# A fused decoder layer on one core: rotations by neighbour DMA and GpSimd, masks by ScalarE and GpSimd, half of the convolution's taps as matmuls

## The reference, cut to what matters

```python
# block 1 (state space), D_INNER = 256, D_STATE = 16
x_b, z = split(x @ W_in)
xc = silu(conv_b + sum_k xpad[:, k:k+T, :] * conv_w[:, k])       # four taps, causal, within a sequence
delta = softplus(proj[..., :8] @ W_dt + b_dt); B_in, C_in = proj[..., 8:24], proj[..., 24:]
h = exp(delta * A) * h + delta * B_in * xc                       # a scan over T, per channel and state
y = (sum_s h * C_in + D_param * xc) * silu(z); x1 = layernorm(x + y @ W_out)
# block 2 (retention): queries from x1, keys and values from ctx
rot(u) = stack(-u[1::2], u[0::2]); q = (x1 @ Wq) * cos + rot(x1 @ Wq) * sin; k likewise, with 1/scale
x2 = layernorm(x1 + (q @ k.T * decay_mask) @ (ctx @ Wv))
# block 3 (experts): top 2 of 16, hidden = silu(gate) * up, plus a shared expert
out = layernorm(x2 + combine * experts(x2) + shared(x2))
```

## Time and profile before

| | |
|---|---|
| median of three runs | 1300.01 us |
| the profiled execution, its own time | 1300.71 us |
| its span in the trace | 1298.7 us |
| mean granted TensorE clock | 0.962 of full |
| busy: VectorE / TensorE / ScalarE / GpSimd | 1174.9 / 1065.3 / 939.8 / 897.3 us |
| mean busy share of the 16 DMA engines | 42.4% |

### The profile page before, as it was taken

The page is one execution under the profiler, slowest core; times in us unless marked ns, Lnnn a source line. Parts: engine busy times, 40 slices in busy tenths (PEclk is TensorE's granted clock), DMA queues, the critical chain, the costliest instruction groups (busy, mean ns, idle before and its releaser), DMA issues. The chain is left out here.

```text
span 1298.7 us, 18075 instructions
## 1 busy us (share of the span) xinstructions
PE 1065.3 (82%) x5959; PEld 733.0 (56%) x5959; DVE 1174.9 (90%) x1185; ACT 939.8 (72%) x2183; POOL 897.3 (69%) x556
## 2 busy tenths in 40 slices
PE   4476788888898878888887988888798888978877
PEld 2344455656565565656655665655666565556654
DVE  1999999999999999999999999999999999999621
ACT  4567768877777878777777787777778777777432
POOL 0567667778687777778767787877777787778533
PEclk7669799999999999999999999999999999999989
DMA  7334243343544444445444444454444444444112
GB/s 177 141 104 168 100 163 133 127 174 132 180 144 167 136 148 150 144 168 172 142 159 145 145 149 152 165 170 149 131 150 145 160 153 169 143 143 166 40 45 73
DMA packets 77149, 185.83 MB, mean 143 GB/s; under 512 B 15848, under 2 KB 43904, under 8 KB 60672
## 3 DMA queue, kind: packets, MB, share of 16 engines
q1 hardware_dynamic: 77056, 184.68, 42.4%
HBM read 178.88 MB, written 5.77 MB: 142 GB/s over the span
## 5 line engine op out<-in xcount | busy, mean ns | idle before, releaser
L811 POOL TENSOR_TENSOR read<-state,bc_all 128x1024 f32<-128x1024 f32 x256 | 603.5, 2360 | 258.7 <-DVE state L761 257.3
L761 DVE TENSOR_TENSOR_SCAN state<-decay,drive_bank 128x1024 f32<-128x1024 f32 x256 | 584.5, 2283 | 12.4 <-POOL read L811 0.3
L606 ACT ACTIVATE decay<-delta,a_neg 128x252 f32<-128x252 f32 x1024 | 422.8, 496 | 0.6
L244 PE MATMUL y_bank<-ident,read 128*128 128x128 f32 x2048 | 282.6, 283 | 85.2 <-POOL read L811 84.9
L644 DVE TENSOR_TENSOR drive_bank<-dx_bank,bc_all 128x1024 f32<-128x1024 f32 x256 | 314.8, 1230 | 24.6 <-DMA bc_all<-bc_dram 14.7
L244 PEld LDWEIGHTS y_bank<-ident,read 128*128 128x128 f32 x2048 | 237.3, 145 | 163.0 <-POOL read L811 139.1
L840 POOL TENSOR_TENSOR hid<-gu,comb_all 128x512 f32<-128x512 f32 x128 | 162.3, 1274 | 34.7 <-DVE gu L776 17.4
L583 ACT ACTIVATE silu<-bank 128x512 f32<-128x512 f32 x144 | 85.7, 595 | 135.7 <-PE bank L240 134.4
L240 PE MATMUL bank<-x2T,up_w 128*128 128x512 f32 x256 | 133.8, 604 | 16.7 <-DVE conv L616 12.7
L240 PEld LDWEIGHTS down_bank<-down_w,hid 128*128 128x128 f32 x1024 | 127.7, 193 | 34.8 <-issue 26.8
L240 PE MATMUL down_bank<-down_w,hid 128*128 128x128 f32 x1024 | 138.6, 279 | 3.7 <-POOL hid L840 1.7
(11 more groups left out here) (123 smaller groups left out, 1418.4 us busy)
## 6 DMA issues: line engine op xcount, KB each, us to landing
bc_all<-bc_dram SPq DMA_DIRECT2D x128, 1024.0 KB, 5.0
comb_all<-comb_dram SPq DMA_DIRECT2D x256, 128.0 KB, 5.0
x_in<-in_x_dram SPq DMA_DIRECT2D x16, 256.0 KB, 5.4
ctx_in<-in_ctx_dram SPq DMA_DIRECT2D x16, 256.0 KB, 5.3
out_dram<-y_out SPq DMA_DIRECT2D x16, 256.0 KB, 2.6
bc_dram<-proj SPq DMA_DIRECT2D x16, 64.0 KB, 4.3
gate_w<-in_L_ffn_gate_proj_dram SPq DMA_DIRECT2D x1, 512.0 KB, 4.7
up_w<-in_L_ffn_up_proj_dram SPq DMA_DIRECT2D x1, 512.0 KB, 6.6
```

The costliest lines, as they stand in the source:

```text
L244: return e.matmul(out, in_, identity[0:n, 0:n], is_transpose=True, start=start, stop=stop, skip_group_check=True)
L606: done = e.activation(seqs(decay_t[j % DECAYS][:, i, h, :])[:, :, 1:T], seqs(delta[c % 2][:, h, sub * SUB:(sub + 1) * SUB])[:, :, 1:T], AC ...
L761: e.tensor_tensor_scan(flat(state_t[j % STATE_BUFS][:, :, :, :]), flat(decay_t[j % DECAYS][:, :, :, :]), flat(drive_bank[:, :, :, :]), 0.0 ...
L811: e.tensor_tensor(read_t[j % READS][:, :, :, :], state_t[j % STATE_BUFS][:, :, :, :], bc_all[group % BC_BUFS][:, 1, PAIR * i:PAIR * (i + 1 ...
```

## The change

It removes `w_swap` and its copies, the second k and q matmuls, the five VectorE multiplications of rotations and mask, and the VectorE taps of channels 0 to 127. In their place: ScalarE copies k, q and the scores out of PSUM. SyncE exchanges neighbouring partitions of k and q by two DMAs each (64 partitions x 2 KB). GpSimd multiplies k and q in place (128x1024 each) and the scores by the mask (128x512). Four matmuls with weights scaled by the taps compute the first half's convolution, from whose PSUM tile silu reads directly. The taps of one channel half are loaded, broadcast over the partitions, by a sixth DMA of `first_consts`. `w_out` and `down_w` are loaded before the other late weights and centred at slot -1. The neighbour DMAs stand on SyncE's queue at 30 (k) and 42 (q).

Places that move: on TensorE xT -24 to -23, proj -16 to -15, ctxT 30 to 29, v 33 to 32, out 36 to 37, x1T 43 to 41, score 52 to 50, retout 53 to 55, router 65 to 62. On ScalarE ctxT 31 to 29, squares and normalise of the first norm 35 to 36 and 39 to 40, x1T 44 to 42, x2T 61 to 60, gate_z 5 and 25 to 4 and 24, delta -8 to -9, the router's exp 66 to 65, the last norm one later. On VectorE the router's second pick 66 to 67 and its end 68 to 67, so that the wait for the exp follows directly behind the difference that the exp reads. On GpSimd the norms' scales 39 to 38 and 55 to 56, dx -9 to -6. On SyncE bc_dram -10 to -11, comb_dram 67 to 65, the x load -59 to -67, the ctx load 26 to 16, the output 95 to 96. The second half's taps stand at -18, -18 and -17.

```diff
+        w_tap = sb("w_tap", [P, TAPS, P])
-        w_swap = sb("w_swap", [P, 2, D])
-        conv = sb("conv", [P, HALVES, CHUNK])
+        conv = sb("conv", [P, CHUNK])
+        tap_rows = read_t[0][:, :, :, :].rearrange("p i h n -> p (i h n)")[:, 0:P * TAPS]
-        EXP_AT = [11, 28]
+        EXP_AT = [11, 27]
-        FFN_AT = [70, 72, 73, 74, 78, 84, 86, 87, 90]
+        FFN_AT = [70, 71, 72, 74, 78, 84, 86, 87, 90]
...
+                if (c := chunk_at(slot, -21)) is not None:
+                    bank = take(("xb", c, 0), slot, 1.5)
+                    w.wait_ge(S["xT"], at(c))
+                    w.wait_ge(S["w_tap"], 1)
+                    for n in range(TAPS):
+                        done = mm(seqs(bank.t[:, :])[:, :, n:T], w_tap[:, TAPS - 1 - n, :],
+                                  seqs(xT[c % 3][:, :])[:, :, 0:T - n], start=n == 0, stop=n == TAPS - 1)
+                    done.then_inc(S["xb_mm"], 1)
+                    bank.free = (S["xc"], at(c, 0, HALVES))
...
-                for i in range(2):
-                    if (c := chunk_at(slot, 34 + i)) is not None:
-                        bank = take(("k", c, i), slot, 1.5)
...
+                if (c := chunk_at(slot, 30)) is not None:
+                    bank = take(("k", c), slot, 1)
...
+                    mm(bank.t[:, :], w_qkv[:, 1, :], ctxT[:, :]).then_inc(S["k_mm"], 1)
+                    bank.free = (S["k_copy"], at(c))
...
+                if (c := chunk_at(slot, 42)) is not None:
+                    bank = take(("q", c), slot, 1)
...
+                if (c := chunk_at(slot, 31)) is not None:
+                    w.wait_ge(S["k_mm"], at(c))
+                    w.wait_ge(S["k"], at(c - 1))
+                    copy(k_pair[:, 0, :], bank_of["k", c][:, :]).then_inc(S["k_copy"], 1)
...
+                if (c := chunk_at(slot, 42)) is not None:
+                    w.wait_ge(S["q_mm"], at(c))
+                    w.wait_ge(S["q"], at(c - 1))
+                    copy(q_pair[:, 0, :], bank_of["q", c][:, :]).then_inc(S["q_copy"], 1)
+                if (c := chunk_at(slot, 49)) is not None:
+                    w.wait_ge(S["score_mm"], at(c))
+                    w.wait_ge(S["retout_mm"], at(c - 1))
+                    copy(ret[:, :, :], blocks(bank_of["score", c][:, :])).then_inc(S["ret_copy"], 1)
...
-                    e.activation(xc[c % 2][:, :, :], conv[:, :, :], ACT.Silu, scale=1.0).then_inc(S["xc"], 1)
+                    e.activation(xc[c % 2][:, 0, :], bank_of["xb", c, 0][:, :], ACT.Silu, bias=conv_b[:, 0:1],
+                                 scale=1.0).then_inc(S["xc"], 1)
...
+                    e.activation(xc[c % 2][:, 1, :], conv[:, :], ACT.Silu, scale=1.0).then_inc(S["xc"], 1)
...
+            e.tensor_tensor(w_tap[:, :, :], w_in[:, 0:P].unsqueeze(1).to_broadcast([P, TAPS, P]),
+                            tap_rows.rearrange("p (n k) -> p k n", k=TAPS), ALU.mult).then_inc(S["w_tap"], 1)
...
+                        (0, -1, ((w_out[:, :, :], 0, HALVES), (down_w[:, :, :], HALVES, PAIRS))),
+                        (1, 3, ((w_qkv[:, 2:3, :], HALVES + PAIRS, 1), (shared_w[:, 2:3, :], HALVES + PAIRS + 1, 1)))):
...
-                if (c := chunk_at(slot, 68)) is not None:
+                if (c := chunk_at(slot, 67)) is not None:
                     w.wait_ge(S["top_exp"], at(c))
...
+                if (c := chunk_at(slot, 39)) is not None:
+                    w.wait_ge(S["k_swap"], at(c, 1, 2) * 16)
+                    pair = k_pair[:, :, :].rearrange("p i (b t) -> p i b t", t=T)
+                    e.tensor_tensor(pair, pair, xpos[:, 2:4, :].unsqueeze(2).to_broadcast([P, 2, CHUNK_SEQS, T]),
+                                    ALU.mult).then_inc(S["k_rot"], 1)
+                if (c := chunk_at(slot, 44)) is not None:
...
+                    e.tensor_tensor(k_t[:, :], k_pair[:, 0, :], k_pair[:, 1, :], ALU.add).then_inc(S["k"], 1)
+                if (c := chunk_at(slot, 46)) is not None:
+                    w.wait_ge(S["q_swap"], at(c, 1, 2) * 16)
...
+                if (c := chunk_at(slot, 47)) is not None:
...
+                if (c := chunk_at(slot, 52)) is not None:
+                    w.wait_ge(S["ret_copy"], at(c))
+                    e.tensor_tensor(ret[:, :, :], ret[:, :, :], decay_mask[:, :].unsqueeze(1).to_broadcast([P, BLOCKS, P]),
+                                    ALU.mult).then_inc(S["ret"], 1)
...
+                if (c := chunk_at(slot, 30)) is not None:
+                    w.wait_ge(S["k_copy"], at(c))
+                    for side in (0, 1):
+                        e.dma_start(k_pair[side:P:2, 1, :], k_pair[1 - side:P:2, 0, :]).then_inc(S["k_swap"], 16)
+
+                if (c := chunk_at(slot, 42)) is not None:
+                    w.wait_ge(S["q_copy"], at(c))
+                    for side in (0, 1):
+                        e.dma_start(q_pair[side:P:2, 1, :], q_pair[1 - side:P:2, 0, :]).then_inc(S["q_swap"], 16)
```

More of the change, by code:

```diff
@@ L304, in _ @@
                     bank.free = (S["flip_copy"], 3)
-                if (c := chunk_at(slot, 30)) is not None:
+                if (c := chunk_at(slot, 29)) is not None:
                     bank = take(("ctxT", c), slot, 1)
@@ L445, in _ @@
                         continue
+                    w.wait_ge(S["centered"], 2)
                     if index == 0:
@@ L654, in _ @@
                                         ALU.mult).then_inc(S["y_gated"], 1)
[L656 to L673 removed]
+                if (c := chunk_at(slot, -18)) is not None:
+                    tap(c, 1)
+                if (c := chunk_at(slot, -18)) is not None:
+                    tap(c, 2)
+                if (c := chunk_at(slot, -17)) is not None:
+                    tap(c, 3)
+                for part, at_slot, centered in (
+                        (0, -1, ((w_out[:, :, :], 0, HALVES), (down_w[:, :, :], HALVES, PAIRS))),
+                        (1, 3, ((w_qkv[:, 2:3, :], HALVES + PAIRS, 1), (shared_w[:, 2:3, :], HALVES + PAIRS + 1, 1)))):
+                    if slot != at_slot:
+                        continue
+                    if part == 0:
+                        w.wait_ge(S["out_consts"], 16 * 2)
+                    else:
+                        w.wait_ge(S["flip_copy"], 2)
+                    first, last = centered[0][1], centered[1][1] + centered[1][2]
                     for weights, i, n in centered:
@@ L888, in _ @@
             for slot in range(FIRST, LAST + 1):
-                if (c := chunk_at(slot, -10)) is not None:
+                if (c := chunk_at(slot, -11)) is not None:
                     w.wait_ge(S["proj"], at(c))
```

211 lines of the change are left out of this document (87 added, 124 removed).

## The result

The changed kernel takes 1277.0 us (median of 4 runs, 1275.4 to 1278.4) where the kernel before took 1300.1 (4 runs), a ratio of 0.982 with a 95% interval of 0.980 to 0.984. It is faster by 23 us, 1.8%; forecast were 55, and the time lies above the range. The profiled execution took 1275.4 us, its span 1273.6.

The account below looks back on a forecast made before the run. VectorE was taken to set the period. From 1300.7 us, minus 73.5 (its gain) and 3.4 (slot 3), plus 2.3 (start), 7 (router), 12 (crowding) and 0 (tail), came 1245 us; range 1226 to 1273.

Parts of the forecast that it names:

- VectorE's gain: Per chunk, taps, rotation multiplications and mask leave VectorE's queue: 4.9 us a chunk, 73.5 us over 15 chunks.
- the exchange and GpSimd: Neighbour DMAs of k and q land in 4 us, hidden, costing nothing; GpSimd's rotation products last 2.36 us without DMA waits.
- slower by q's exchange: Rival: ScalarE copies q late, GpSimd stands at slot 46 and VectorE waits in turn; 1320 us, chance 0.04.
- the router: VectorE's wait for the exp directly behind the difference: 0.45 us a chunk, 7 us lost.
- Where it collides: Crowding of TensorE (slots 20 to 27) and GpSimd (5 to 17): 0.8 us a chunk, 12 us lost; bounds nothing and 3.
- TensorE or GpSimd becomes the bound: Rival: in-order queues at 88 to 92% cannot keep up; chunk 71.0 to 73 us, time 1258 to 1288, chance 0.24.
- once, at slot 3: Before the second scan, VectorE's swap copies vanish and weight sums and subtractions move to slot -1: 3.4 us gained.
- The start: Before the first scan, more conv matmuls and a sixth constants DMA: 2.3 us lost, bounds 0.5 and 5.
- The tail: After the last scan, two fewer TensorE matmuls against q's longer way: 0 taken, within 3 us.

Follow-up runs that it names:

- a_no_gp_mult: Changed kernel with GpSimd's two rotation products (k and q) left out: 1272.4 us.
- h_act_less: Changed kernel with half of ScalarE's decay exps left out (one state of each pair gets no decay): 1246.4 us.
- l_start: Changed kernel with ScalarE's conv bias waiting only for its own matmul, first-half silu for both, and flipped-weight copies at slot -1: 1270.3 us, ratio to before 0.976.
- p_dt_start: l_start with the dt matmuls over 40 rows instead of 8, the added weights being zero: 1260.1 us, ratio to before 0.969.
- n_exp_28: Changed kernel with the second group of decays from slot 28 on, as before the change, not 27: 1294.2 us, ratio to before 0.994.
- r_mask_back: Changed kernel with the mask on VectorE again, without ScalarE's copy of the scores and GpSimd's mask product: 1281.0 us.
- f_taps_on_dve: Changed kernel with the first half's three taps back on VectorE and one matmul in place of four: 1335.2 us.
- g_before_tap_mm: Kernel before the change with the first half's four tap matmuls alone, everything else where it was: 1348.1 us.
- s_fill_dt_start: p_dt_start with two 512-column filler matmuls in TensorE's wait for the second y_gated: 1262.4 us.

## Why the prediction was wrong

**Right: VectorE's gain, nearly.** From scan to scan, the six stretches that lose work or get the router's take 34.6 us before and 29.7 after, the exp's 0.27 taken off: 4.8 us less, and 4.9 were forecast. (Period less recorded waits gives only 4.4, because a product that waits costs about 0.12 us beyond its recorded wait: from scan to scan with one product between are 4.09 us without a wait and 5.04 with one of 0.84. The 73.8 us taken for a period was a window a little short of one; the sum used differences alone and doesn't suffer, but "69.3" should have been 70.5.)

**Right: the exchange and GpSimd.** The rotation products take 2.36 and 2.37 us, and no wait for a DMA stands before them:
```profile
L844 POOL TENSOR_TENSOR q_pair<-q_pair,xpos 128x1024 f32<-128x1024 f32 x16 | 37.9, 2368 | 0.0
L835 POOL TENSOR_TENSOR k_pair<-k_pair,xpos 128x1024 f32<-128x1024 f32 x16 | 37.8, 2362 | 0.0
```
a_no_gp_mult shows that the added work costs nothing. The rival "slower by q's exchange" had no part in it. TensorE's 66.1 us a chunk were some 2 above the forecast.

**Right: the router**, 0.27 us a chunk where 0.45 was taken.

**Wrong: "Where it collides".** This is the step that failed: the term of 12 us, 0.8 a chunk, with 3 as its bound. Measured were 2.7 us a chunk of waits less the exp's 0.27, so 2.4, or 36 us in 15 chunks; with the 0.12 behind each it is 2.9, or 44 us, about the bound. With the bound of 3 in the sum it gives 1278, yet the range was closed at 1273. Three things in it were wrong.
- It laid TensorE's and GpSimd's work beside VectorE's, slot by slot, and left ScalarE out, because that engine had 16 us idle a chunk. Yet in the stretch from the q projection to slot 21 it was 95% busy already before, and half its decays gone return 29 us (h_act_less); of the 31.9 us in the two `gu` rows, 19.6 name its silu. The stretch was nearly as long as ScalarE's list, and most of VectorE's 2.0 us there could not come off it. Half a microsecond of the wait at slot 15 is the change's own making: ScalarE's bias waits in every chunk for the four tap matmuls, which it does not need (l_start).
- TensorE was looked at from slot 20 to 27 only. Of VectorE's waits for it one, at slot 27, lies there; the other is at slot 11, and near 15 ScalarE and TensorE wait for each other (the rows in l_start), which no count of one engine's work shows.
- The clock was taken as full, as it is in the middle before. With the new order it fell behind the dt matmuls in some chunks. In the changed kernel the wait at slot 27 is 0.24 us above the 0.27 that is left with 40 rows, 4 us in 15 chunks; in l_start, which brings the fall more often, it is 10 us (against p_dt_start).

By the time alone the rival "TensorE or GpSimd becomes the bound" (1258 to 1288) came nearest, but its engine was wrong in part: ScalarE with TensorE, and GpSimd not at all.

**Wrong: once, at slot 3.** The 3.4 us of copies and sums went, but they were given back. VectorE's timeline there, changed kernel, beside the earlier trace rows:
```profile
33.41 2.29 DVE L769 TENSOR_TENSOR_SCAN state<-decay,drive_bank 128x1024 f32<-128x1024 f32 x1
35.73 1.23 DVE L673 TENSOR_TENSOR drive_bank<-dx_bank,bc_all 128x1024 f32<-128x1024 f32 x1
40.77 0.29 DVE L703 TENSOR_REDUCE row_sum<-w_qkv 128x1 f32<-128x128 f32 x1 [3.80 <-ACT shared_w L476]
...
41.89 2.28 DVE L769 TENSOR_TENSOR_SCAN state<-decay,drive_bank 128x1024 f32<-128x1024 f32 x1
```
The wait for ScalarE's copies grew from 1.01 to 3.80 us, as they stand behind a run of 20 exps (31.98 to 39.98), four of which the move from slot 28 to 27 put ahead of them: with 28 (n_exp_28) the wait is 2.22 us. The rest is that ScalarE comes to that run 1.9 us later than before. l_start takes the copies out from behind it, and the second scan follows 5.2 us after the first: the forecast's "some 5.6". The reckoning was right for VectorE and left out what ScalarE had queued, the same omission.

**The start** lost 0.7 us in this execution and up to 4.2 in others with the same start; 2.3 were taken, with bounds of 0.5 and 5. (The low clock that the prediction takes for the first passes is worked out from their 0.91 us each; the clock column gives 1.00 for that stretch.) The bias waited 6.2 us for all five matmuls of the conv, though it needs the first; with that mended the first scan comes 1.0 us earlier than before the change. **The tail** changed by 0.5, 0 was taken.

**The sum by measured terms:** 15 x 4.8 = 72 gained, 41 of new waits lost between 100 and 1190 us and some 7 (an estimate, 59 products at 0.12) behind them, 0.7 lost at the start, 0.5 gained at slot 3 (8.48 against 9.0) and 0.5 at the tail: 24 us, against 25 between the two spans.

What stays open: how ScalarE's and TensorE's parts divide where both are late, since h_act_less takes 12 us a chunk (194 of ScalarE's busy time) and with them the lateness of all that queues behind; whether the wait at slot 21 is the copy of the scores (r_mask_back); and what the tap matmuls are worth, as neither f_taps_on_dve nor g_before_tap_mm prices them alone. A version that moves ScalarE's table loads, rather than its decays, wasn't tried.

## What to carry to other kernels

Before crediting a saving on the engine that bounds, cut a period at instructions that every engine passes, and read the busy share of *every* engine in each piece: an engine with 16 us to spare in a period can be 95% busy in the piece where the saving falls, and then only a part of the saving comes through. With in-order queues and shared banks, the runs here that took work off GpSimd, TensorE or VectorE gave 5 to 11 us, while moving a copy, a pick or a group of exps by one slot cost 17 to 24 us; so look in its own queue, at what stands directly ahead of it and what it frees. And look for what waits longer than it needs: two such waits and 32 rows of zeros gave 17 us, almost as much as the change.

## What was not expected of the hardware

- TensorE's granted clock fell to 0.50, the 1.2 GHz level, behind four passes of 8-row matmuls, with only 0.63 us of wait a little ahead of them and the engine busy otherwise (n_exp_28, in many chunks but not in all). With 40 rows in their place VectorE's wait behind them is 0.27 or 0.28 us in each of twelve chunks, so it did not fall there, the passes themselves being no faster (2.03 us both), and the mean of that wait went from 1.03 (l_start) to 0.28 us (p_dt_start). The Trainium skill ("TensorE: Matmul & The Clock Gate", Part 1) says that a gate sets the clock by how busy TensorE has been; this trace agrees in so far as TensorE's 2.15 us of wait ahead of `y_gated` is followed by the low level too, as the window 535.5 to 538.5 of the changed kernel shows:
```profile
535.50:538.50 3.00, 3.00 (x15) 2.91 (x14) 2.39 (x13) 1.19 (x5) 0.62 (x1) 0.50 0.00 0
```
- A low clock need not cost the kernel anything that shows: filling the wait at `y_gated` raised the mean clock from 0.947 to 0.955 and gave no time (s_fill_dt_start against p_dt_start, 1262.4 and 1260.1 us).
- A DMA of 128 KB within SBUF landed in 2.0 us (median of 32, for k and for q), half of the 4 us taken, where loads of that size from DRAM in the same loop took 4.8. The rule that the prediction cites (the Trainium skill, "DMA: Bandwidth & Descriptors", Anatomy of one DMA) makes it 2.3 us, an estimate: the section gives it for DMAs issued from GpSimd, and these are SyncE's. The quiet row of before said 2.3 as well, and both were nearer than the 4:
```profile
comb_all<-comb_dram SPq DMA_DIRECT2D x256, 128.0 KB, 4.8
...
k_pair<-k_pair SPq DMA_DIRECT2D x32, 128.0 KB, 2.0
q_pair<-q_pair SPq DMA_DIRECT2D x32, 128.0 KB, 2.0
```
